# Attention scores of the two head parities on separate row halves of TensorE, and sixteen groups without a loop

## The reference

```python
q = q * cos + _rotate_half(q) * sin
k = k * cos + _rotate_half(k) * sin
qg = q.reshape(b, HKV, G, t, DH)
scores = jnp.einsum('bhgtd,bhkd->bhgtk', qg.astype(jnp.float32), k.astype(jnp.float32)) / math.sqrt(DH)
causal = jnp.tril(jnp.ones((t, t), dtype=bool))
scores = jnp.where(causal[None, None, None], scores, jnp.finfo(jnp.float32).min)
attn = jax.nn.softmax(scores, axis=-1).astype(x.dtype)
ctx = jnp.einsum('bhgtk,bhkd->bhgtd', attn, v)
```

## Time and profile before

| what | us |
|---|---|
| median of three runs | 1794.19 |
| profiled execution, span | 1792.7 |
| TensorE matmul busy | 1521.2 (85%) |
| VectorE busy | 1148.1 (64%) |
| ScalarE busy | 607.1 (34%) |
| items, line 1594: first and last start | 1141.9 to 1681.7 |
| transposed scores, line 1612: first and last start | 1174.2 to 1712.6 |
| mean granted TensorE clock | 0.904 |

### The profile page before, as it was taken

The page is one execution under the profiler, slowest core; times in us unless marked ns, Lnnn a source line. Parts: engine busy times, 40 slices in busy tenths (PEclk is TensorE's granted clock), DMA queues, the critical chain, the costliest instruction groups (busy, mean ns, idle before and its releaser), DMA issues. The chain is left out here.

```text
span 1792.7 us, 24031 instructions
## 1 busy us (share of the span) xinstructions
PE 1521.2 (85%) x7034; PEld 1036.6 (58%) x7034; DVE 1148.1 (64%) x2429; ACT 607.1 (34%) x859; POOL 340.2 (19%) x382
## 2 busy tenths in 40 slices
PE   0399889898846881999999999699999999999969
PEld 0366657566535660777777776355555555555447
DVE  5576875768645455455555543688687786888527
ACT  4224223242223330111111111046456465666632
POOL 2243343334312230000000000012122121121211
PEclk9988979889767895999999999579899898999979
DMA  7200000100023432100000000402112111211032
GB/s 263 94 1 1 24 24 1 47 1 24 1 89 125 150 124 89 30 25 18 24 25 18 15 9 0 87 8 48 28 27 54 27 27 27 54 27 29 2 131 82
DMA packets 48596, 84.12 MB, mean 47 GB/s; under 512 B 8899, under 2 KB 16657, under 8 KB 48506
## 3 DMA queue, kind: packets, MB, share of 16 engines
q1 hardware_dynamic: 41874, 78.13, 15.0%
q10 hardware_dynamic: 6632, 4.97, 0.9%
HBM read 58.54 MB, written 24.26 MB: 46 GB/s over the span
## 5 line engine op out<-in xcount | busy, mean ns | idle before, releaser
L1515 ACT ACTIVATE f_prob<-f_bank 128x1024 f32<-128x1024 f32 (+3 forms) x384 | 304.4, 811 | 216.6 <-PE f_bank L1612 214.5
L1594 PE MATMUL f_bank<-f_kst,f_qst 96*128 96x512 f32 (+3 forms) x768 | 282.8, 412 | 24.9 <-DMA f_qst<-q_scr 12.5
L1535 DVE CUSTOM_DVE_ANT_0 f_bank<-f_bank,f_mask 128x128 f32<-128x128 f32 (+3 forms) x512 | 248.5, 503 | 79.5 <-PE f_bank L1594 64.0
L1594 PEld LDWEIGHTS f_bank<-f_kst,f_qst 96*128 96x128 f32 x768 | 153.0, 204 | 181.0 <-DVE f_mx L1535 62.3
L1612 PE MATMUL f_bank<-f_qst,f_kst 98*128 98x512 f32 (+3 forms) x768 | 217.0, 367 | 1.2 <-ACT f_prob L1515 1.2
L1483 POOL TENSOR_SCALAR_AFFINE_SELECT f_prob<-f_prob 128x256 f32<-128x256 f32 x256 | 104.0, 407 | 467.8 <-ACT f_prob L1515 467.2
L1538 DVE TENSOR_REDUCE f_mx_first<-f_bank 128x1 f32<-128x512 f32 x256 | 176.1, 688 | 17.4 <-issue 8.1
L1630 PE MATMUL f_bank<-f_prob,f_vst 128*32 128x512 f32 (+3 forms) x1536 | 169.3, 514 | 1.0 <-ACT f_prob L1515 0.8
L37 PE MATMUL d_bank<-xtl,d_wgh 128*128 (+1 forms) x352 | 143.1, 407 | 8.9 <-DMA d_zz<-z_gu_scr 8.9
L1612 PEld LDWEIGHTS f_bank<-f_qst,f_kst 98*128 98x128 f32 x768 | 135.2, 199 | 20.6 <-ACT f_prob L1515 9.3
L1187 ACT ACTIVATE d_hs<-d_bank 128x512 f32<-128x512 f32 (+1 forms) x44 | 26.3, 598 | 348.8 <-PE d_bank L39 348.8
(11 more groups left out here) (225 smaller groups left out, 2761.6 us busy)
## 6 DMA issues: line engine op xcount, KB each, us to landing
f_qst<-q_scr SPq DMA_DIRECT2D x32, 384.0 KB, 6.1
q_scr<-c_qh SPq DMA_DIRECT2D x32, 256.0 KB
wst<-L_ffn_w SPq DMA_DIRECT2D x6, 1024.0 KB, 6.5
f_kst<-k_scr SPq DMA_DIRECT2D x32, 192.0 KB, 5.2
d_qw<-L_ffn_qweight_gu SPq DMA_DIRECT2D x40, 128.0 KB, 2.6
xall<-L_attn_x SPq DMA_DIRECT2D x2, 2048.0 KB, 16.2
xb<-L_attn_x SPq DMA_DIRECT2D x4, 1024.0 KB, 5.6
x_d<-xb SPq DMA_DIRECT2D x4, 1024.0 KB, 4.3
```

Source lines behind the costliest of these rows:

```text
L1515: act.activation(prob[:, c // 2 % 2, c % 2 * 2:c % 2 * 2 + 2, lo:], score_bank[c % 2][:, :, lo:], ACT.Exp, scale=D ** -0.5).then_inc(exp_d ...
L1535: dve.tensor_tensor_reduce(sc, sc, mask[:, CH - w:CH], 1.0, LEAST, ALU.add, ALU.max, mx[:, u, h % 2, h // 2, q:q + 1]).then_inc(spare_free, 1)
L1594: pe.matmul(spare[v][:, 0:w], qst[0:M_ROW, u, h // 2, q * P:q * P + P], kst[0:M_ROW, u, h % 2, at:at + w], start=True, stop=True).then_inc ...
```

## The change

It has these parts.

1. The parities stand on halves of the array: rows 0 to 47 and 64 to 111, with the maximum of each in row 48 and row 112. A transposed product takes only the 49 rows of its own parity in place of all 98. An item takes rows 0 to 111.
2. Row 48 is now inside an item's rows, so it has to be zero while items of a group are made: each load gets a fifth DMA, of one row of zeros, and `qst` is cleared at the start by VectorE.
3. `ITEMS` is ordered by pairs: the same queries and keys' span for the even head and then for the odd head. Widths and their number stay.
4. The loops of all engines are gone; the 16 groups are written out.

```diff
-M_ROW = 2 * PART
+HALF_ROWS = P // 2
...
-ITEMS = [(h, q, at, min(CH, (q + 1) * P - at)) for h in range(HG) for q in range(QB) for at in range(0, (q + 1) * P, CH)]
+ITEMS = [(2 * i + par, q, at, min(CH, (q + 1) * P - at)) for i in range(HG // 2) for q in range(QB)
+         for at in range(0, (q + 1) * P, CH) for par in range(2)]
+
+
+def stack_rows(par, extra=0):
+
+    return slice(par * HALF_ROWS, par * HALF_ROWS + PART + extra)
...
-LOADED = 4 * 16
+LOADED = 5 * 16
+ITEM_ROWS = HALF_ROWS + PART
...
-            for c in range(HEAD):
-                run(c, 0, 0, True)
-            with eng.Fori(0, ROUNDS - 1) as j:
-                for k in range(STACKS):
-                    for c in range(HEAD, NC):
-                        run(c, j, k)
-                    for c in range(HEAD):
-                        run(c, j, k + 1)
-            for n in range((ROUNDS - 1) * STACKS, NG):
-                for c in range(HEAD if n == (ROUNDS - 1) * STACKS else 0, NC):
-                    run(c, 0, n)
+            for n in range(NG):
+                for c in range(NC):
+                    run(c, 0, n, n == 0 and c < HEAD)
...
-                    r = slice(par * PART, par * PART + PART)
+                    r = stack_rows(par)
...
+                sp.dma_start(qst[PART:PART + 1, u].bitcast(F32), kst[P - 1:P, 0].bitcast(F32)).then_inc(qk_in[u], 16)
...
+                dve.tensor_scalar(qst[:, u], fixed[:, :, :].broadcast_to([P, HG // 2, T]), 0.0, None, ALU.mult)
...
-                pe.matmul(spare[v][:, 0:w], qst[0:M_ROW, u, h // 2, q * P:q * P + P],
-                          kst[0:M_ROW, u, h % 2, at:at + w], start=True, stop=True).then_inc(spare_ps, 1)
+                pe.matmul(spare[v][:, 0:w], qst[0:ITEM_ROWS, u, h // 2, q * P:q * P + P],
+                          kst[0:ITEM_ROWS, u, h % 2, at:at + w], start=True, stop=True).then_inc(spare_ps, 1)
...
-                    mm = pe.matmul(score_bank[c % 2][:, hh, lo:], kst[0:M_ROW + 2, u, hh, k * P:k * P + P],
-                                   qst[0:M_ROW + 2, u, c % 2, h * CH + lo:(h + 1) * CH], start=True, stop=True)
+                    r = stack_rows(hh, 1)
+                    mm = pe.matmul(score_bank[c % 2][:, hh, lo:], kst[r, u, hh, k * P:k * P + P],
+                                   qst[r, u, c % 2, h * CH + lo:(h + 1) * CH], start=True, stop=True)
```

More of the change, by code:

```diff
@@ L1346, in layer1_attention @@
         fixed = sb("fixed", [P, 2, 1])
-        qst = sb("qst", [P, STACKS, 2, T], F32R)
+        qst = sb("qst", [P, STACKS, HG // 2, T], F32R)
         kst = sb("kst", [P, STACKS, 2, T], F32R)
@@ L1368, in layer1_attention @@
         NI = len(ITEMS)
-        ROUNDS = (NG - 1) // STACKS
         def span(h, k):
@@ L1447, in maxima @@
                 for par in range(2):
-                    sp.dma_start(qst[M_ROW + par:M_ROW + par + 1, u].rearrange("o i (b q) -> o (i b) q", q=P).bitcast(F32),
+                    row = par * HALF_ROWS + PART
+                    sp.dma_start(qst[row:row + 1, u].rearrange("o i (b q) -> o (i b) q", q=P).bitcast(F32),
                                  mt[par * 2 * QB:(par + 1) * 2 * QB, u].bitcast(F32)).then_inc(m_in[u], 16)
@@ L1461, in _ @@
             maxima(group(0, 0), True)
[L1462 to L1466, removed]
+            for n in range(NG - 1):
+                step(group(0, n), group(0, n + 1), group(0, n + STACKS) if n + STACKS < NG else None)
         @block.gpsimd
@@ L1884, in shape_constants @@
     fixed = np.zeros((P, 2, 1), f)
-    fixed[M_ROW, 0], fixed[M_ROW + 1, 1] = -1, -1
+    fixed[PART, 0], fixed[HALF_ROWS + PART, 1] = -1, -1
     c["fixed_d"] = fixed
```

## The result

The kernel after takes 2048.22 us, the median of four executions (2018.94 to 2066.02), against 1793.97 us for the kernel before: a ratio of 1.130, with a 95% interval of 1.125 to 1.135. Its executions spread more than those of before, and all go with the clock: their mean granted clock is 0.808, 0.801, 0.785 and 0.783. The ratio and its interval rest on the two shortest; the two medians as they stand would give 1.142.

What follows compares the result with a forecast made beforehand. TensorE was taken to bound a group, at 32.2 us against VectorE's 25.6. Forecast: 1792.7 - 29.5 (loop) + 67.2 (pairs) + 1.5 (clearing) = 1831.9, with 1.5 for the median 1833.4 us; range 1785 to 1885.

Steps and rivals of the forecast that it cites:

- The loop written out: Attention's group loop: removing its three slow turns gains 29.5 us, or 0 if new code stalls as much.
- The rival's "code" half: Written-out groups: code read only once stalls, the 29.5 us don't come, 1863 us; chance 0.05 together with a falling clock.
- The pair's block: Two half-height transposed products between full-height ones: 0.64 us per block at 512 columns, 5.2 us a group more on TensorE.
- 1.0 swallowed: TensorE's waits in a group: 1.0 of the 5.2 us hidden by shrinking waits for VectorE, leaving +4.2, 67 us in all.
- The free change: Shape changes between halves and full height cost nothing, a group loses 4.2 us on TensorE: 1715 us; chance 0.15.
- the serial loads: The pair's second weights load only after the first's, 0.10 us each, 38 us more: 1871 us; chance 0.16 with no overlap.
- no overlap: The two halves of a pair don't run side by side, 67 us more: 1900 us; chance 0.16 with serial loads.
- more swallowed: Waits hide more of the pair's 5.2 us: half showing gives 1808 us, a third 1794; chance 0.12.
- The items in pairs: Items over 112 rows, equal widths twice in a row for VectorE: three banks cover it, 0, within 5 us either way.
- The clearing: VectorE's three added clearing instructions before the first load: the stage starts 1.5 us later.
- The clock: TensorE's granted clock: fell after a 2.6 us pause; shape changes leave 0.1, so a fall was given little chance.
- a rival of 0.05 in all: Written-out code stalls or the clock falls, so the loop's 29.5 us don't come: 1863 us; chance 0.05.

Runs made afterwards that it cites:

- e1: The kernel before with only its loops written out as 16 groups: 1761.25 us, ratio 0.982.
- e3: The kernel after with both transposed products of a pair on the even half's 49 rows, so one follows the other: 2296.13 us, ratio 1.281.
- e10: The kernel after with 64-row halves for items and transposed products, a sixth DMA and the item order of the kernel before: 1744.59 us, ratio 0.974.
- e2: The kernel after with transposed products over all 113 rows in place of 49-row halves: 1789.8 us, ratio 0.997.
- e8: The kernel of e2 with the items in the order of the kernel before: 1761.4 us, ratio 0.983.
- e6: The kernel after with transposed products over all 64 rows of a half in place of 49, the added rows zeros: 1885.1 and 1916.62 us.
- e12: The kernel after with the items in the order of the kernel before, 49 rows kept: 1881.91 us, ratio 1.049.
- e11: The kernel after with 64 rows of a half in transposed products and the item order of the kernel before: 1838.11 us, ratio 1.026.
- e5: The kernel after with the items on 48-row halves too: 1875.65 us, ratio 1.048.
- e9: The kernel after with 64-row halves for both items and transposed products and a sixth DMA, pairs' order kept: 1763.03 us, ratio 0.986.
- e4: The kernel of e2 with a product of 48 rows and two columns added before every second pair: 1849.53 us, ratio 1.031.
- e7: The kernel of e2 with a product of 48 rows and two columns added before every pair: 1980.26 us, ratio 1.104.

## Why the prediction was right in sign and wrong in size

**The loop written out, -29.5: right.** e1 measured 32.7, and no code stalls came in the turns' place. The rival's "code" half fell.

**The pair's block, 0.64 us, +5.2 a group: its parts right, its sum somewhat high.** The starts are 3 to 4 ns apart, the item's load follows the pair's by 0.44 us where 0.44 was computed, and loads start with their matmuls. The Trainium skill ("TensorE: Matmul & The Clock Gate", Part 3) has about 4 ns between such starts, and the trace agrees with 3 to 4. The Trainium skill ("TensorEngine Tiling (Array Packing)", Key Properties) says that a changed tiling mode drains the engine; the trace agrees, as the loads at 1242.47 and 1242.91 start with their matmuls and not ahead of them. At full clock the halves cost 37.3 - 33.8 = 3.5 us a group in the pairs' order, 35.3 - 31.9 = 3.4 in the other. The prediction had 5.2 less 1.0 swallowed, 4.2. So 55 us in place of 67.

**The free change, the serial loads, no overlap, more swallowed: fell as rivals.** e3 shows that the overlap exists and is worth about what was said (4.1 to 4.6 us a group by estimate, 4.2 said). The free change is what e10 comes near to, by having no change of shape: 1744.6, though not 1715, since VectorE is in the way sooner.

**The items in pairs, "three banks cover it. 0, within 5 us either way": wrong.** e2 against e8 measured 28 us. The step took three banks for cover; items in pairs sat idle for 10.7 of 400 us, against 0.2. Because of it the group of 36.4 us that the prediction named and the 37.3 worked out agree only in part for the right reason: 32.2 + 4.2 against 31.9 + 1.9 + 3.5.

**The clearing, +1.5: not more than that.** The clearing takes 1.22 us, and e8 is level with e1.

**The clock, "The clock fell after a pause of 2.6 us; changes of shape leave 0.1, so I give it little": this step failed, and it is most of the error.** The account of the profiled spans: 1792.7, less 33 for the loop (e1's span is 1759.7), plus 30.5 for the order (e2's 1790.2), plus 55 for the halves at full clock, is 1845; what is left to 2017.2 is about 172 us. Of it 148 us lie between the third and the last marker (633.0 less 13 groups of 37.3), in groups all or part of whose time is at the 1.2 GHz level. The median execution adds 29 us (2048.22 - 2018.94) at a clock lower still. The prediction had the clock as one half of a rival of 0.05 in all, whose 1863 us is the price of stalling code alone; a fallen clock had no price. I had read from the loop's turn that a pause lowers the clock, and concluded that without a pause it would hold. The trace of before could not show that products over few rows lower it, since it had none in such number.

What lowers it is told by pairs of runs that differ in one edit:

- Rows: after and e6 (49 and 64 rows): 387 of 633 us at half clock against 89 of 517. e12 and e11, the same in the other order: 121 of 509 against 0 of 459. e5 and e9, where all scores are on halves (48 or 49 rows, and 64; e9 has a sixth DMA too): 328 of 511 against 31 of 415.
- Short products of another shape: e2, e4, e7 (0, 12, 24 added to a group, all real score products with 112 rows or more): 0, 17 and 140 us. From e6 to e9, where the items lose rows too (112 to 64) but keep the pairs' shape: 89 to 31.
- Order of the items, and with it the waits for VectorE: after and e12: 387 against 121.

The experiments ran on four chips, on each of which the kernel before took 1789.5 to 1794.6 us. After itself was not run again beside e6 or e12, so that the chip has a part in where a kernel tips is not excluded; it could not make e5, e6 and e7 differ, which shared one.

Rows alone can't be the cause: e7 falls with all real score products at 112 rows or more. Changes of shape alone can't either: e6 has those of after and a quarter of its time at half clock. That the three have one thing in common, fewer cells of the array at work per microsecond, would be the obvious sum, and it fails here. By rows times columns a group of e10 is about two thirds of one of e7 (64 rows for 112 or 113, the weighed sums alike) in three quarters of the time (30.4 of 40.7 us), so fewer cells are at work, and yet it is at half clock for 14 of 402 us where e7 is for 140 of 591.

Where the clock falls can be read. In the kernel after, TensorE's timeline before its fall at 1261.26:

```profile
1258.83 0.42 PE L1630 MATMUL f_bank<-f_prob,f_vst 128*32 128x128 f32 x8
1259.18 0.82 PE L1593 MATMUL f_bank<-f_kst,f_qst 112*128 112x128 f32 x2
1260.49 0.28 PE L1600 MATMUL f_bank<-f_ident,f_mx 128*32 128x128 f32 x1 [0.49 <-DVE f_mx L1534]
1260.71 0.50 PE L1612 MATMUL f_bank<-f_qst,f_kst 49*128 49x512 f32 x2
```

It is the place that e6 showed. From the second marker to the last, after, e3, e4, e6, e7, e9 and e10 have 47 falls of the clock to its lower level, and 40 of them come within 1.8 us after the start of the transpose of the maxima (after: 7 of 9); of e5's 14 none does. The same place stands in e1, e2, e8, e11 and e12, whose clock doesn't fall in this time, so it isn't enough by itself. No run moves the transpose or fills the wait before it, which would be the next thing to try.

The Trainium skill ("TensorE: Matmul & The Clock Gate", A second HAM failure mode) tells of short idle times between groups of matmuls that let the clock go to and fro. The going to and fro is in these traces, and the falls stand behind a wait of about half a microsecond; the amount of idle time doesn't order the runs. From 1250 to 1650 us TensorE is idle for 4.1 us in e7 at a clock of 0.85, for 4.0 in after at 0.68, for none in e3 at 0.51, and for 43.3 in e9 at 0.96. Nor does it cover that zeros in 15 more rows bring the clock back. How the chip draws the line stays open.

## What to carry to other kernels

A product on part of the rows between full-height products pays for two changes of shape; compute emptying and reload from a row of the same kind, and either give all neighbours the same shape and all 64 rows of it (e10, -2.6% against before, of which the written-out loop alone is -1.8%) or leave it. The same shape alone isn't enough: e5, with 48 and 49 rows, is 4.8% slower than before. When an edit halves the rows in use, forecast the time at both levels of the granted clock, and look at the clock by stretches first: filling up with rows of zeros cost nothing at full clock and took 134 us off here. An order that gives the consumer equal sizes in a row can cost waits that the mean load doesn't show, 1.9 us a group here; price it by a run of its own.

## What was not expected of the hardware

- Rows of zeros count: from 49 to 64 rows per half, the 15 more all zero, the time at half clock fell from 387 to 89 us.
- TensorE busy in 400 of 400 us had the lowest clock of all, 0.51 (e3), and TensorE idle for 43.3 of them had 0.96 (e9).
- The clock falls nearly always at one place of the group, right behind the transpose of the maxima: 40 of 47 falls in seven kernels.
- A level can stay for long under the same instructions: in e12 three groups in a row take 60.08 us, and nine of the next eleven 35.27 or 35.28.
- A product of 48 rows and two columns between full-height ones costs 0.25 to 0.29 us, though it streams almost nothing; how much of it one over full height would cost, no run shows.
